# Reading expert and batch numbers one at a time in a LoRA and top-2 MoE kernel

## The chip, the cores and the metric

The kernel runs on one core of one Trainium2 chip. The metric is the device time of one execution in microseconds (us); lower is better. It is given as the median of several executions. One more execution was recorded by the hardware profiler, and all durations below come from it.

## The reference

`x` is [16 batches, 128 rows, 128 features], `cond_8` is [16, 8]. The first layer adds to x a linear layer plus a mixture of eight rank-16 adapters weighted by `cond_8`. The second is a mixture of eight gated MLPs (128 to 512 to 128), of which each batch takes the two with the largest softmax weight, plus a shared one:

```python
x = x + (x @ W_base.T + b_base + 2.0 * lora(x, As, Bs, w=cond_8))

def _gemma_mlp(x, gate_w, up_w, down_w):
    g = jnp.einsum('bsh,hi->bsi', x, gate_w)
    u = jnp.einsum('bsh,hi->bsi', x, up_w)
    return jnp.einsum('bsi,ih->bsh', jax.nn.gelu(g, approximate=True) * u, down_w)

rw = softmax(cond_8)
w, sel = top_k(rw, 2); w = w / w.sum()
dense_w = zeros((16, 8)).at[arange(16)[:, None], sel].add(w)
moe = sum(dense_w[:, e] * _gemma_mlp(x, skill_gate[e], skill_up[e], skill_down[e]) for e in range(8))
out = x + moe + _gemma_mlp(x, shared_gate, shared_up, shared_down)
```

## The kernel before

The program writes each engine's instruction stream by hand, and the engines meet only through counting semaphores. Which batch goes to which expert is known only on the chip. The kernel therefore sorts the 32 pairs (batch, expert) into a list, `idx`, in on-chip memory: entries 0 to 31 are expert numbers, entries 32 to 63 batch numbers. VectorE writes it (L758) and then raises the semaphore `lists_ready` to 2. An engine that needs such a number reads it into a register: `down_at` (L229, an expert number times a stride) and `batch_at` (L232). In the trace each such read is a TENSOR_LOAD on the engine's own instruction sequencer, followed by register operations and an assertion.

The work comes in this order.

1. Setup and the first layer.
2. The shared MLP over four groups of four batches (`shared_group(g)`, L969). Step `c` of a group makes one 128-wide piece of gate and up (`gate_up_shared`, six matmuls of 512 columns) and then the down product of two pieces earlier (`down_shared`, three matmuls). In the last group TensorE reads four expert numbers, `first`, after the last gate and up.
3. Four "singles" (pairs that found no partner): `gate_up_single(s)` is 16 matmuls, `down_single(s)` is eight and needs the expert number `first[s]`. TensorE reads four more numbers, `last`, for the four singles at the very end, two before `down_single(1)` and two before `down_single(2)`.
4. Twelve "slots", each two batches of one expert. Slots 0 to 2 are written out, 3 to 11 are a loop of three turns (L1101). A slot has two halves, n = 0 and n = 1. In each half TensorE does `gate_up_slot` (12 matmuls of 256 columns) and then `down_slot` of the same half of the slot before (six).
5. Four last singles, the merge of the sums, and the output.

Tile t is one half of a slot. ScalarE takes its gelu (L533) and later rounds the product to its high part (L542). VectorE multiplies gelu and up (`gated`, L697), and then subtracts to get the low part (`split_h_lo`, L714). In half n it does `gated(t)` first and then `split_h_lo(t - 1)`. `down_slot` of a half waits for that half's low part (`lo_done`, L1040). So in half 1 of slot p TensorE waits for the split that VectorE makes in half 0 of slot p, and in half 0 of slot p + 1 for the split made in half 1 of slot p. VectorE also reads the two batch numbers of the previous slot in half 0 (`where`, L791), after the split, and adds that slot's result in half 1 (`add_slot`, L780).

SyncE copies the gate and up weights of a slot from `wex` to `wst`, both in on-chip memory, 1024 KB at a time (L284), once the slot three before has left its buffer.

VectorE's stream around the first singles is `gated_single(1)`, `add_single(0)`, two reads, `gated_single(2)`, `add_single(1)`, two reads, `gated_single(3)`, `add_single(2)`, `add_single(3)`, two reads, and then slot 0. `down_single(s)` waits for `gated_single(s)`.

Of the kernel before, what the change touches and what calls it, by code (L numbers as in the profile page):

```python
# [17 lines left out]
def lora_then_top2_moe(nc, x, cond, W_base, b_base, As, Bs, ex_gate, ex_up, ex_down,  # L18
# [8 lines left out]

    B, S, H = x.shape
    E, _, I = ex_gate.shape
    R = As.shape[1]  # L30
    P = 128
    assert S == P and H == P and E * R == P and I == 512
    GB = I // S
    NG = B // GB
    NC = I // P
# [4 lines left out]
    NU = NG * NC  # L40
    NP = 12
    NF, NL = 4, 4
    NS = NF + NL
    PB = NU + NF
    LB = PB + 2 * NP
    LEFT = 2 * NP
    NBUF = 3
    RT_WEIGHTS = 11

    with ExitStack() as ctx:  # L50
# [3 lines left out]
        def sem(name):  # L54
            return ctx.enter_context(nc.semaphore(name))
# [127 lines left out]
        lists_ready = sem("lists_ready")  # L183
# [39 lines left out]
        def split_count(t):  # L223

            return t + (1 - NF)

        def down_at(eng, n):

            return eng.snap(eng.value_load(idx[0:1, bass.ds(n, 1)], min_val=0, max_val=E - 1) * DN)  # L229

        def batch_at(eng, n):
            return eng.value_load(idx[0:1, bass.ds(n + 32, 1)], min_val=0, max_val=B - 1)  # L232
# [373 lines left out]
        def _(dve):  # L606
# [86 lines left out]
            def gated(t, q, u):  # L693

                dve.wait_ge(up_done, t + 1)
                dve.wait_ge(gelu_done, t + 1)
                dve.tensor_tensor(up_ps[u][:, :], up_ps[u][:, :], gelu_sb[q], ALU.mult).then_inc(h_done, 1)  # L697

            def gated_single(s):
                t = SINGLES[s]  # L700
                dve.wait_ge(up_done, t + 1)
                dve.wait_ge(gelu_done, t + 1)
                if s >= 2:
                    dve.wait_ge(down_done, SINGLES[s - 2] + 1)
                dve.tensor_tensor(h_sb[t % 2], up_ps[t % 3][:, :], gelu_sb[t % 2], ALU.mult).then_inc(h_done, 1)  # L705

            def split_h_lo(t, q, u, count):

                dve.wait_ge(hi_done, count)
                if isinstance(t, int) and PB <= t < PB + 2:  # L710
                    dve.wait_ge(down_done, NU)
                elif not (isinstance(t, int) and t < 2):
                    dve.wait_ge(down_done, t - 1)
                dve.tensor_tensor(hT_lo[:, q, :], up_ps[u][:, :], f32(hT_hi[:, q, :]), ALU.subtract).then_inc(lo_done, 1)  # L714
# [56 lines left out]
            def batches_of(p):  # L771
                return [batch_at(dve, 2 * p + n) for n in range(2)]

            def add_slot(p, j, where):

                dve.wait_ge(down_done, 2 * p + (PB + 2))
                dve.wait_ge(acc_done, 2 * p + NF)
                for n in range(2):
                    of_b = total[:, bass.ds(where[n], 1), :].rearrange("p a s -> p (a s)")
                    dve.scalar_tensor_tensor(of_b, slot_ps[j][:, n * S:(n + 1) * S], wlist[:, bass.ds(2 * p + n, 1)],  # L780
                                             of_b, ALU.mult, ALU.add).then_inc(acc_done, 1)

            def slot(p, j):
                adds = not (isinstance(p, int) and p == 0)
                for n in range(2):
                    t = 2 * p + (PB + n)
                    gated(t, n, (PB + 2 * j + n) % 3)
                    if adds or n == 1:
                        split_h_lo(t - 1, 1 - n, (PB + 2 * j + n - 1) % 3, split_count(t - 1))
                    if adds and n == 0:  # L790
                        where = batches_of(p - 1)  # L791
                    if adds and n == 1:
                        add_slot(p - 1, (j + 2) % NBUF, where)

# [19 lines left out]
            gate_lo(E - 1)  # L814
            sum_group(NG - 1)
            first = [batch_at(dve, LEFT + s) for s in range(2)]
            gated_single(1)
            add_single(0, first[0])
            first += [batch_at(dve, LEFT + s) for s in range(2, NF)]
# [2 lines left out]
            last = [batch_at(dve, LEFT + s) for s in range(NF, NF + 2)]  # L822
            gated_single(3)
            add_single(2, first[2])
            add_single(3, first[3])
            last += [batch_at(dve, LEFT + s) for s in range(NF + 2, NS)]
            dve.wait_ge(sum_done, NG)
            for p in range(NBUF):
                slot(p, p)
            with dve.Fori(1, NP // NBUF) as i:  # L830
                for j in range(NBUF):
                    slot(NBUF * i + j, j)
            where = batches_of(NP - 1)
            split_h_lo(LB - 1, 1, (LB - 1) % 3, split_count(LB - 1))
            gated_single(NF)
            add_slot(NP - 1, (NP - 1) % NBUF, where)
            gated_single(NF + 1)
            for g in range(NG):
                merge(g)
# [8 lines left out]
        def _(pe):  # L848
# [101 lines left out]
            def down_shared(g, c):  # L950

                q = c % 2
                pe.wait_ge(lo_done, NC * g + (c + 1))
                if c == 0:
                    if isinstance(g, int) and g == 0:
                        pe.wait_ge(x1_ready, 2)
                        pe.wait_ge(sh_dlo, 1)
                    else:
                        pe.wait_ge(sum_done, g)
                w_hi = wshd[:, 0, c, :]  # L960
                w_lo = wshd[:, 1, c, :]
                pe.matmul(shared_ps[:, :], w_hi, hT_hi[:, q, :], start=(c == 0), stop=False)  # L962
                pe.matmul(shared_ps[:, :], w_hi, hT_lo[:, q, :], start=False, stop=False)
                pe.matmul(shared_ps[:, :], w_lo, hT_hi[:, q, :], start=False, stop=(c == NC - 1)  # L964
                          ).then_inc(down_done, 1)

            first = []

            def shared_group(g):  # L969
                for c in range(NC):  # L970
                    gate_up_shared(g, c)
                    if NC * g + c == NU - 1:
                        pe.wait_ge(lists_ready, 2)
                        first.extend(down_at(pe, LEFT + s) for s in range(NF))
                    if g == 0 and c == 2:
                        sort_starts()
                    if g == 1 and c == 2:
                        sort_singles()
                    if g == 2 and c == 3:
                        sort_lists()  # L980
                    if c >= 2:
                        down_shared(g, c - 2)
                    elif g > 0:
                        down_shared(g - 1, c + 2)

            def gate_up_single(s):

                t = SINGLES[s]
                j = s % NBUF
                pe.wait_ge(xs_ready, s + 1)  # L990
                pe.wait_ge(st_gu[j], 32 * (s // NBUF) + 32)
                pe.wait_ge(h_done, t - 1)
                if s < 3:
                    pe.wait_ge(lo_done, t - 2)
                elif NF <= s < NF + 3:
                    pe.wait_ge(lo_done, split_count(t - 3))
                for k, ps, done in ((0, gate_ps[t % 2], gate_done), (1, up_ps[t % 3], up_done)):
                    for c in range(NC):
                        mm = pe.matmul(ps[:, c * S:(c + 1) * S], sst[:, j, k * I + c * P:k * I + (c + 1) * P],  # L999
                                       xs[:, s % NBUF, :], start=True, stop=True)  # L1000
                    mm.then_inc(done, 1)

            def down_single(s, e0):

                t = SINGLES[s]
                if s in (2, 3):
                    pe.wait_ge(acc_done, s - 1)
                elif s == NF + 1:
                    pe.wait_ge(merged, 3)
                elif s == NF + 2:  # L1010
                    pe.wait_ge(res_done, 1)
                elif s == NF + 3:
                    pe.wait_ge(merged, NG)
                pe.wait_ge(h_done, t + 1)
                for c in range(NC):
                    mm = pe.matmul(single_ps[s][:, 0:H], h_sb[t % 2][:, c * S:(c + 1) * S],  # L1016
                                   wexd[:, bass.ds(e0 + c * H, H)], start=(c == 0), stop=(c == NC - 1))
                mm.then_inc(down_done, 1)
# [66 lines left out]
                shared_group(g)  # L1085
            pe.wait_ge(ld_down, 32)
            gate_up_single(0)
            down_shared(NG - 1, NC - 2)
            down_shared(NG - 1, NC - 1)
            gate_up_single(1)  # L1090
            down_single(0, first[0])
            gate_up_single(2)
            last = [down_at(pe, LEFT + s) for s in range(NF, NF + 2)]
            down_single(1, first[1])
            gate_up_single(3)
            last += [down_at(pe, LEFT + s) for s in range(NF + 2, NS)]
            down_single(2, first[2])
            down_single(3, first[3])
            for p in range(NBUF):
# [46 lines left out]
```

## Time and profile before

| | |
|---|---|
| median of 3 executions | 135.22 us (134.91 to 135.67) |
| the profiled execution | 135.5 us, span from first to last instruction 133.8 us |
| TensorE matmul busy | 127.2 us, 95% of the span, 869 matmuls |
| VectorE busy | 88.7 us, 66% |
| ScalarE busy | 70.9 us, 53% |
| GpSimd busy | 60.2 us, 45% |
| granted TensorE clock, whole span | 1.00 (2.4 GHz) |

The span leaves out 1.7 us of the execution's own 135.5 us. Matmul intervals overlap in the records: a matmul of 256 columns lasts 0.28 us, but in an undisturbed row the next one starts 0.12 us after it, one of 512 columns 0.23 us. So an idle TensorE is best seen from the distance between two starts. Register reads are not counted as busy time of any engine; they stand in the chain as DVEq (VectorE's sequencer) or, where the profile names nothing, as "issue".

### The profile page before, as it was taken

The numbers are of one execution on the slowest core, as the hardware profiler recorded it, in microseconds if no ns is written. First come the engines' busy times: TensorE is split into PE (matmuls) and PEld (weight loads), VectorE is DVE, ScalarE is ACT, GpSimd is POOL, SyncE is SP. The second block draws the span as 40 slices with busy tenths as digits, with TensorE's granted clock in tenths as the row PEclk, the third lists the DMA queues.
The fourth block names the chain that finished last, engine by engine and source line by source line (L and its number), as shares of the span: only waits on it lengthen the run. The fifth ranks groups of instructions, "written<-read, shape, count | busy, mean of one in ns | idle before, by whom it ended". The sixth has DMA issues, their size and how long they took to land.

```text
span 133.8 us, 3280 instructions
## 1 busy us (share of the span) xinstructions
PE 127.2 (95%) x869; PEld 114.2 (85%) x869; DVE 88.7 (66%) x172; ACT 70.9 (53%) x134; POOL 60.2 (45%) x110
## 2 busy tenths in 40 slices
PE   6899999999999989996999999999999999999991
PEld 6658787878878869995999999999989999989991
DVE  2668978779977888533376658656855686756732
ACT  3432867976876766120466485657554755711110
POOL 5209384497777644632064543554255504610000
DMA  3898878798000185599345686558799940013822
GB/s 51 245 335 290 287 197 300 227 308 247 12 2 0 39 266 170 157 394 409 144 174 218 238 316 240 193 201 313 260 316 322 347 167 0 0 41 121 248 85 61
DMA packets 14526, 26.56 MB, mean 199 GB/s; under 512 B 2225, under 2 KB 7601, under 8 KB 12977
## 3 DMA queue, kind: packets, MB, share of 16 engines
q1 hardware_dynamic: 14192, 26.35, 58.8%
q8 instruction: 5, 0.08, 0.2%
q10 hardware_dynamic: 320, 0.07, 0.2%
q14 instruction: 9, 0.07, 0.2%
HBM read 12.52 MB, written 1.31 MB: 103 GB/s over the span
## 4 chain that ended last, share of the span: by engine, by line
PE 78%; DVEq 6%; DVE 4%; issue 4%; DMA 3%; ACT 2%; SPq 0%; ACTq 0%
PE bank L999 8%; PE bank L1036 7%; PE bank L1035 7%; PE bank L1034 7%; PE bank L946 5%; PE bank L948 5%; PE bank L947 5%; DVEq L232 5%; PE bank L1016 5%; PE bank L1056 4%; PE bank L962 3%; PE bank L1058 3%; PE bank L1057 3%; PE bank L871 3%; PE bank L964 3%
## 5 line engine op out<-in xcount | busy, mean ns | idle before, releaser
L533 ACT ACTIVATE work<-bank 128x512 f32<-128x512 f32 x48 | 28.7, 598 | 43.0 <-PE bank L1036 18.3
L697 DVE TENSOR_TENSOR bank<-bank,work 128x512 f32<-128x512 f32 x40 | 27.9, 697 | 23.2 <-PE bank L1036 12.5
L714 DVE TENSOR_TENSOR hT_lo<-bank,hT_hi 128x512 fp32r<-128x512 f32 x40 | 27.3, 682 | 1.7 <-issue 0.8
L1034 PE MATMUL bank<-xp,wst 128*128 128x256 f32 x96 | 27.2, 284 | 0.0
L1035 PE MATMUL bank<-xp,wst 128*128 128x256 f32 x96 | 27.2, 283 | 0.0
L1036 PE MATMUL bank<-xp,wst 128*128 128x256 f32 x96 | 27.1, 283 | 0.0
L463 POOL TENSOR_TENSOR wstd<-wexd,wstd 128x512 fp32r<-128x512 f32 x12 | 15.5, 1295 | 23.8 <-ACT wstd L575 23.8
L542 ACT CAST hT_hi<-bank 128x512 fp32r<-128x512 f32 x40 | 23.3, 582 | 2.4 <-DVE bank L697 1.3
L1035 PEld LDWEIGHTS bank<-xp,wst 128*128 128x128 f32 x96 | 18.4, 192 | 0.0
L1036 PEld LDWEIGHTS bank<-xp,wst 128*128 128x128 f32 x96 | 18.4, 192 | 0.0
L1034 PEld LDWEIGHTS bank<-xp,wst 128*128 128x128 f32 x96 | 18.4, 192 | 0.0
L999 PE MATMUL bank<-xs,sst 128*128 128x128 f32 x128 | 15.6, 275 | 0.0
L999 PEld LDWEIGHTS bank<-xs,sst 128*128 128x128 f32 x128 | 15.1, 192 | 0.2
L1056 PE MATMUL bank<-hT_hi,wstd 128*128 128x256 f32 x48 | 14.4, 301 | 0.6 <-DVE hT_lo L714 0.5
L456 POOL CAST xp<-x1s 128x256 fp32r x24 | 9.6, 398 | 11.1 <-issue 10.1
L1058 PE MATMUL bank<-hT_hi,wstd 128*128 128x256 f32 x48 | 13.6, 283 | 0.0
L1057 PE MATMUL bank<-hT_lo,wstd 128*128 128x256 f32 x48 | 13.6, 282 | 0.0
L371 POOL TENSOR_TENSOR wex<-raw_ex,wex 128x512 fp32r<-128x512 f32 x8 | 10.3, 1288 | 6.3 <-DVE wex L719 6.3
L946 PE MATMUL bank<-x1s,wsh 128*128 128x512 f32 x32 | 12.6, 393 | 0.0
L948 PE MATMUL bank<-x1s,wsh 128*128 128x512 f32 x32 | 12.5, 390 | 0.0
L947 PE MATMUL bank<-x1s,wsh 128*128 128x512 f32 x32 | 12.5, 389 | 0.0
L705 DVE TENSOR_TENSOR work<-bank,work 128x512 f32<-128x512 f32 x8 | 5.5, 690 | 8.4 <-PE bank L999 5.8
(146 smaller groups left out, 212.7 us busy)
## 6 DMA issues: line engine op xcount, KB each, us to landing
wst<-wex SPq DMA_DIRECT2D x12, 1024.0 KB, 5.0
raw_ex<-n_L_cond_skill_gate_dram SPq DMA_DIRECT2D x8, 256.0 KB, 3.3
raw_ex<-in_L_cond_skill_up_dram SPq DMA_DIRECT2D x8, 256.0 KB, 4.2
sst<-n_L_cond_skill_gate_dram SPq DMA_DIRECT2D x8, 256.0 KB, 3.4
sst<-in_L_cond_skill_up_dram SPq DMA_DIRECT2D x8, 256.0 KB, 4.2
xn<-in_x_dram SPq DMA_DIRECT2D x4, 256.0 KB, 4.6
out_dram<-xT SPq DMA_DIRECT2D x4, 256.0 KB, 2.7
sst<-_L_cond_shared_gate_dram SPq DMA_DIRECT2D x1, 256.0 KB, 4.6
```

Source lines behind the costliest of these rows:

```text
L533: act.activation(gelu_sb[q], gate_ps[q][:, :], ACT.Gelu_apprx_tanh).then_inc(gelu_done, 1)
L542: act.copy(hT_hi[:, q, :], up_ps[u][:, :]).then_inc(hi_done, 1)
L697: dve.tensor_tensor(up_ps[u][:, :], up_ps[u][:, :], gelu_sb[q], ALU.mult).then_inc(h_done, 1)
L714: dve.tensor_tensor(hT_lo[:, q, :], up_ps[u][:, :], f32(hT_hi[:, q, :]), ALU.subtract).then_inc(lo_done, 1)
L946: pe.matmul(ps[:, :], w_hi, x1_hi(g), start=True, stop=False)
L947: pe.matmul(ps[:, :], w_hi, x1_lo(g), start=False, stop=False)
L948: pe.matmul(ps[:, :], w_lo, x1_hi(g), start=False, stop=True).then_inc(done, 1)
L999: mm = pe.matmul(ps[:, c * S:(c + 1) * S], sst[:, j, k * I + c * P:k * I + (c + 1) * P], xs[:, s % NBUF, :], start=True, stop=True)
L1034: pe.matmul(of_c, w_hi, x_hi, start=True, stop=False)
L1035: pe.matmul(of_c, w_hi, x_lo, start=False, stop=False)
L1036: mm = pe.matmul(of_c, w_lo, x_hi, start=False, stop=True)
L1056: pe.matmul(ps, w_hi, h_hi, start=(c == 0), stop=False)
```

## The change

The numbers read and the arithmetic are the same. Only the places of the reads in two instruction streams move.

- TensorE, last shared group: in place of four reads after the last `gate_up_shared`, one read after each of the steps c = 1, 2 and 3 (with the wait for the list in front of the first), and the fourth after `gate_up_single(0)`.
- TensorE, singles: the four reads of `last` stand one each after `gate_up_single(1)`, `down_single(0)`, `gate_up_single(2)` and `down_single(1)`.
- VectorE, slots 1 to 11: the first of the two reads of `where` moves from behind `split_h_lo` to between `gated` and `split_h_lo` of half 0. The second stays behind the split.
- VectorE, ends: the last two reads of `last` move from before slot 0 into slot 0, half 0, behind `gated`. The two reads for the last slot (`last_slot`) move from behind the loop into slot 0, half 1.

```diff
@@ VectorE, slot(p, j) @@
                     gated(t, n, (PB + 2 * j + n) % 3)
+                    if adds and n == 0:
+                        where = [batch_at(dve, 2 * p - 2)]
                     if adds or n == 1:
                         split_h_lo(t - 1, 1 - n, (PB + 2 * j + n - 1) % 3, split_count(t - 1))
                     if adds and n == 0:
-                        where = batches_of(p - 1)
+                        where.append(batch_at(dve, 2 * p - 1))
+                    elif n == 0:
+                        last.extend(batch_at(dve, LEFT + s) for s in range(NF + 2, NS))
+                    elif not adds:
+                        last_slot.extend(batches_of(NP - 1))
@@ VectorE, around the slots @@
+            last_slot = []
             gated_single(1)
...
             add_single(3, first[3])
-            last += [batch_at(dve, LEFT + s) for s in range(NF + 2, NS)]
...
-            where = batches_of(NP - 1)
             split_h_lo(LB - 1, 1, (LB - 1) % 3, split_count(LB - 1))
             gated_single(NF)
-            add_slot(NP - 1, (NP - 1) % NBUF, where)
+            add_slot(NP - 1, (NP - 1) % NBUF, last_slot)
@@ TensorE, shared_group(g) @@
                     gate_up_shared(g, c)
-                    if NC * g + c == NU - 1:
-                        pe.wait_ge(lists_ready, 2)
-                        first.extend(down_at(pe, LEFT + s) for s in range(NF))
+                    if g == NG - 1 and c >= 1:
+                        if c == 1:
+                            pe.wait_ge(lists_ready, 2)
+                        first.append(down_at(pe, LEFT + c - 1))
@@ TensorE, singles @@
             gate_up_single(0)
+            first.append(down_at(pe, LEFT + NF - 1))
             down_shared(NG - 1, NC - 2)
             down_shared(NG - 1, NC - 1)
             gate_up_single(1)
+            last = [down_at(pe, LEFT + NF)]
             down_single(0, first[0])
+            last.append(down_at(pe, LEFT + NF + 1))
             gate_up_single(2)
-            last = [down_at(pe, LEFT + s) for s in range(NF, NF + 2)]
+            last.append(down_at(pe, LEFT + NF + 2))
             down_single(1, first[1])
+            last.append(down_at(pe, LEFT + NF + 3))
             gate_up_single(3)
-            last += [down_at(pe, LEFT + s) for s in range(NF + 2, NS)]
             down_single(2, first[2])
```

## Rows read from the trace of the kernel before

**Rows 1.** The page, part 1: busy time and share of the span.

```profile
PE 127.2 (95%) x869; PEld 114.2 (85%) x869; DVE 88.7 (66%) x172; ACT 70.9 (53%) x134; POOL 60.2 (45%) x110
```

**Rows 2.** Timeline of TensorE: start, length, [idle before, releaser].

```profile
44.78 0.39 PE L962 MATMUL bank<-hT_hi,wshd 128*128 128x512 f32 x1
...
49.52 0.49 PE L962 MATMUL bank<-hT_hi,wshd 128*128 128x512 f32 x1 [0.50 <-issue]
...
61.51 1.15 PE L1016 MATMUL bank<-wexd,work 128*128 x8 [0.72 <-issue]
63.01 1.15 PE L1016 MATMUL bank<-wexd,work 128*128 x8 [0.34 <-DVE work L705]
```

**Rows 3.** Timeline of VectorE at the list's last write.

```profile
44.17 0.20 DVE L758 CAST idx<-bank 1x64 int32<-1x64 f32 x1
```

**Rows 4.** TensorE's first read, by its source line: durations in ns.

```profile
L229 PEldq TENSOR_LOAD <-idx x1: 493/493/493, 46.5 to 46.5; - x1
```

**Rows 5.** The chain that ended last, from 56 us on: start, length, what.

```profile
59.51 0.83 DVEq L232
...
60.65 1.00 DVEq L232
...
62.06 0.70 DVE work L705
...
118.38 0.70 DVE hT_lo L714
```

**Rows 6.** Stretches from slot start to slot start: slots 1, 2, 3 to 9, 10, 11.

```profile
66.87:71.45 4.58, 4.56 (x38) 4.36 (x37) 2.58 (x4) 3.31 (x7) 3.18 (x4) 1.00 0.58 224
71.45:75.85 4.40, 4.40 (x39) 4.38 (x37) 3.04 (x7) 2.66 (x5) 2.10 (x3) 1.00 0.65 244
75.85:107.32 31.47, 31.10 (x254) 30.44 (x253) 21.02 (x42) 19.18 (x35) 14.59 (x21) 1.00 0.75 269
107.32:111.95 4.63, 4.58 (x39) 4.38 (x37) 3.52 (x7) 2.67 (x5) 1.72 (x2) 1.00 0.28 108
111.95:116.27 4.32, 4.32 (x39) 4.32 (x37) 3.09 (x7) 2.75 (x5) 1.48 (x2) 1.00 0.00 0
```

**Rows 7.** Timeline of all engines in slot 3, which starts at 75.85.

```profile
77.57 0.70 DVE L697 TENSOR_TENSOR bank<-bank,work 128x512 f32<-128x512 f32 x1
...
78.18 0.68 DVE L714 TENSOR_TENSOR hT_lo<-bank,hT_hi 128x512 fp32r<-128x512 f32 x1
...
79.45 0.28 PE L1056 MATMUL bank<-hT_hi,wstd 128*128 128x256 f32 x1
```

**Rows 8.** VectorE's reads of slot 3 (first) and from 109.3 on: min/median/max ns.

```profile
L232 DVEq TENSOR_LOAD <-idx x1: 955/955/955, 78.2 to 78.2; - x1
...
L232 DVEq TENSOR_LOAD <-idx x6: 299/304/313, 109.6 to 117.7; - x6
```

**Rows 9.** ScalarE's seven reads in slots 3 to 9: min/median/max ns.

```profile
L229 ACTq TENSOR_LOAD <-idx x7: 344/674/922, 77.1 to 103.9; - x7
```

**Rows 10.** DMA busy tenths from 75 to 90 us, 0.375 us a digit.

```profile
DMA  9700009989996200299998995100099989994100
```

**Rows 11.** The chain through VectorE's reads of slot 9.

```profile
104.89 0.08 DVEq L232
105.01 0.96 DVEq L232
...
106.38 0.77 DVEq L232
...
107.62 0.07 DVE bank L697
```

**Rows 12.** Timeline of TensorE at the last down_slot.

```profile
118.65 0.28 PE L1058 MATMUL bank<-hT_hi,wstd 128*128 128x256 f32 x1
119.13 0.39 PE L1056 MATMUL bank<-hT_hi,wstd 128*128 128x256 f32 x1 [0.20 <-DVE hT_lo L714]
119.35 0.28 PE L1057 MATMUL bank<-hT_lo,wstd 128*128 128x256 f32 x1
```

## Prediction, written before the changed kernel ran

> **What bounds the kernel now.** I read the page first. TensorE's products are 95% of the span [rows 1], and the granted clock is 1.00 in every stretch of rows 6 (last three columns: clock, DMA share, GB/s). So TensorE sets the end, and a reading counts only where TensorE stands still or comes late. I then went through TensorE's timeline for starts farther apart than 0.23 us (512 columns) or 0.12 us (256), and followed each gap back along the chain.
>
> Three kinds of gap touch the reads. In the last shared group a product starts at 49.52 after 0.50 idle, released by "issue" [rows 2]: TensorE's sequencer was reading four numbers. Its first read starts at 46.5 [rows 4], so four reads took 3.0 us, and products issued before them covered 2.3 of it. At 61.51 there are 0.72 idle for the same reason, and at 63.01 0.34 more, this time released by VectorE's L705. In the chain VectorE does nothing from 59.51 to 62.06 but two reads of 0.83+ and 1.00 us [rows 5]. In the slots, a slot takes 4.32 us when nothing is late (slot 11) and 4.58, 4.40, 31.47 / 7 = 4.50 and 4.63 in slots 1, 2, 3 to 9 and 10 [rows 6]. The excess sits in half 0, where `down_slot` waits for the low part. The last is at 119.13, 0.48 after its neighbour instead of 0.12 [rows 12].
>
> A read's price: its load takes 0.30 us from 109 us on, but 0.955 in slot 3 [rows 8]. Seven first reads of slots 3 to 9 are all long, with a mean of 0.92; the last is the 0.96 of rows 11. The DMA tenths are 9 from 77.3 to 79.9, 81.4 to 84.4 and 86 to 89 us [rows 10]. These are SyncE's 1 MB copies inside on-chip memory, one a slot, and VectorE's first read falls into each. Around the load come 0.12 us before (104.89 to 105.01) and 0.47 after it until the next operation (106.38 + 0.77 = 107.15 to 107.62) in the loop [rows 11]; in written-out code it is 61.65 to 62.06 = 0.41 after it [rows 5].
>
> **TensorE's first read.** The list is ready at 44.17 + 0.20 = 44.37 [rows 3]. The new first read stands ahead of the product due at 44.78 [rows 2] and waits for the list. With TensorE's first load of 0.49 [rows 4] and about 0.41 around it, that product starts at 45.27, 0.49 late. Removed is the gap at 49.52: 0.50 idle plus the 0.16 by which a record of 0.39 outlasts the spacing of 0.23, so 0.66. Each of the two gaps also costs some 0.10 of restart (119.13 to 119.35 is 0.22, not 0.12 [rows 12]), which cancels. Gain **0.17**. Bounds: 0 if the first load takes 0.66, and 0.36 if it takes 0.30.
>
> **TensorE's other seven reads.** I cost them at nothing: each stands behind products already issued, the old run shows that 2.3 us of such cover exists, and a read at its longest is 1.0 + 0.4 = 1.4 us. Without the cover each costs 0.7 to 1.4.
>
> **The middle of the singles.** All of the 0.72 at 61.51 should turn into waiting. `down_single(3)` needs VectorE's L705, which stands behind the two reads from 59.2 to 62.06. Those start when `down_single(1)` is done, which TensorE's own later reads don't move. So the product of 63.01 comes earlier by 0.17 alone, and the 0.88 (0.72 + 0.16) freed before it is spent standing there. Gain **0**; at best about 1.2, if VectorE's two loads fell to 0.3.
>
> **Slots 0 and 1.** VectorE gets four new reads here. Two, behind `gated` in half 0, lie in the time in which ScalarE makes the next gelu: nothing. The other two begin around 67.4 (estimate: slot 1 starts at 66.70, its product ends 0.16 later, and ScalarE's rounding takes another 0.5). Two short reads of 0.30 + 0.41 end at 68.8. Then comes slot 1's own first read, which now stands before the split: 0.92 + 0.41 gives 70.1, and the low part 0.68 + 0.05 later gives 70.85. TensorE wants it at 66.70 + 3.60 + 0.3 (the old wait of half 0, which stays) = 70.6. With restart and the 0.05 that the first half slips, this is a loss of **0.38**. Bounds: 0, and 1.4 if the two reads are long too. Slot 2 (written out, so 0.06 shorter per read) has about 0.05 of lateness and 0.10 of restart where it had 0.08: loss **0.07**.
>
> **Slots 3 to 9, the step that decides.** In half 0 VectorE now does gated, read, split, read. Before, gated started at 77.57, the split at 78.18, and TensorE used that split's result at 79.45 without waiting [rows 7]. After: the load starts at 77.57 + 0.12 = 77.69, inside the copy [rows 10]; + 0.92 + 0.47 = 79.08 for the split; + 0.68 + 0.05 (118.38 + 0.70 = 119.08 to 119.13 [rows 5, 12]) = 79.81. That is 0.36 late, plus 0.10 restart, so 0.46 a slot. The split had 79.45 - 78.18 - 0.73 = 0.54 of slack, and its delay is 0.90. In return the pair of reads starts about 0.5 earlier, gated of half 1 is no later against TensorE, and the old waits of half 0 go. 7 x 0.46 = 3.22 against the old excess 31.47 - 7 x 4.32 = 1.23: loss **1.99**. The copy is issued when half 1's products are done, so TensorE's new wait brings it 0.46 earlier into the slot. The first read stays inside it, and the second may come out of it.
>
> **Slots 10, 11 and the tail.** No copy runs, loads are 0.30 [rows 8], and the split is then 0.28 late, inside the 0.54. Slot 10 loses its excess: gain 4.63 - 4.32 = **0.31**. At the end the split at 118.38 no longer stands behind two reads; 0.36 of gap and 0.10 of restart go: gain **0.46**. TensorE is busy from there to the last single, so both are kept.
>
> **Sum** against the profiled execution: -0.17 + 0.38 + 0.07 + 1.99 - 0.31 - 0.46 = +1.50, so 135.5 + 1.5 = 137.0. The median shown stands 0.28 below that execution: **136.7**, 1.1% more.
>
> **Bounds of the first read.** Nothing in the trace shows VectorE reading that early in a slot. ScalarE reads at 77.1, as the copy begins: 0.34 to 0.92, median 0.67 [rows 9]. With 0.67 a slot costs 0.11 + 0.10 = 0.21 and the sum is about -0.25. With the 1.00 of rows 5 it is about +2.2. I take 0.92, because 77.69 lies as deep in the copy as rows 10 can show.
>
> The Trainium skill (DMA: Bandwidth & Descriptors, Latency and other measured facts) gives a register load a floor of about 600 ns. The 0.30 of rows 8 lies under that floor, so the trace disagrees. By 0.6 in every slot the split would be hardly late, the estimated sum about -1, and the time 134.2.
>
> **Rivals.**
> - The stand-apart works. The early read is short (under 0.92 - 0.36 = 0.56), the split keeps its slack, and the waits of half 0 go: 0.17 + 0.46 + 0.31 + 1.23 + 0.08 = 2.25 less, 133.0. For: loads of 0.30 exist, and ScalarE's shortest is 0.34. Against: seven of seven long. The change pays from a read under about 0.71.
> - The same end by another mechanism: what follows a read need not wait for it. Against: L705 starts at 62.06, right behind a read whose number it does not use [rows 5].
>   The Trainium skill (Advanced Engine Details and Errata, Sequencer Loop) says that other engine instructions can be read and queued while the sequencer executes a control instruction, which would give that. I give it 3 in 100, within the chance of the first rival.
> - Near no change, 135.2: the early read costs like ScalarE's 0.67, or VectorE's two reads in the singles become quick once TensorE does not read beside them (both near 1.0 there), which gives 1.2 back. Against: loads are as long in the slots, with TensorE not reading.
> - Worse, 138: slots 0 and 1 see four long reads in a row (+1.0).
>
> **How the numbers follow.** Forecast (136.0 to 137.6) 0.59, worse 0.08, near no change 0.15, faster 0.18. A measurement tells some 0.5% (0.7 us) from nothing. Slower is the first two, 0.67; same 0.15; faster 0.18. The range is 134.4 to 137.9: it leaves out most of the fast rival and half of the worst one. The forecast's own range is 136.0 to 137.6.
>
> **What would show it.** In the new trace: VectorE's L714 of half 0 starting about 1.5 after L697, not 0.6; TensorE's waits at L1056 in half 1, once a slot, some 0.4, and none in half 0; slots 3 to 9 at 4.78 each; the product near 44.8 coming 0.5 late and none late at 49.5; a wait of 1.4 before `down_single(3)`; no gap at the last `down_slot`. I am wrong if the first load of a slot is short, or if L714 starts while the load still runs.

## The result and the profile after

The changed kernel takes 137.22 us (median of 4, 136.88 to 137.33) against 135.17 us before (4 executions). The ratio is 1.0143, 95% interval 1.012 to 1.0166. The change makes the kernel 1.4% slower; 136.7, 1.1% slower, was forecast. The profiled execution took 137.23 us and has a span of 135.5 us, 1.7 more than before.

The slots come first. These are the same stretches as in [rows 6], from slot start to slot start: slots 1, 2, 3 to 9, 10, 11. The columns are length, busy time of PE, PEld, DVE, ACT and POOL, granted clock, DMA share, GB/s.

```profile
66.73:71.58 4.85, 4.83 (x38) 4.43 (x37) 2.89 (x5) 3.32 (x7) 3.19 (x4) 1.00 0.56 216
71.58:76.06 4.48, 4.48 (x39) 4.38 (x38) 3.51 (x7) 2.67 (x5) 2.09 (x3) 1.00 0.62 234
76.06:109.82 33.76, 32.01 (x254) 30.59 (x253) 22.30 (x43) 18.83 (x35) 14.39 (x21) 1.00 0.73 257
109.82:114.14 4.32, 4.32 (x38) 4.32 (x37) 3.27 (x7) 2.67 (x5) 1.54 (x2) 1.00 0.16 61
114.14:118.46 4.32, 4.32 (x38) 4.32 (x37) 3.20 (x7) 2.74 (x5) 1.65 (x3) 1.00 0.00 0
```

Slots 3 to 9 grew from 31.47 to 33.76 us, and slot 10 shrank from 4.63 to 4.32. The clock is 1.00 throughout, so nothing here is a throttle.

Next, two places on the chain that ended last (start, length, what): VectorE's reads in the singles, which [rows 5] show before, and slot 3, which [rows 7] show.

```profile
59.30 0.91 DVEq L232
...
60.51 1.00 DVEq L232
...
61.93 0.70 DVE work L705
...
77.77 0.08 DVE bank L697
77.85 0.04 issue
77.89 0.98 DVEq L232
...
79.38 0.70 DVE hT_lo L714
80.08 0.04 issue
80.12 0.39 PE bank L1062
```

In slot 3 the read's load starts 0.12 after gated, lasts 0.98, and the split starts 0.51 after its end. L714 now starts 1.61 behind L697, where it was 0.61. The split's product L1062 (L1056 before) starts at 80.12.

TensorE's timeline at the same places, at those of [rows 2], and at the end as in [rows 12]:

```profile
45.23 0.49 PE L967 MATMUL bank<-hT_hi,wshd 128*128 128x512 f32 x1 [0.36 <-DVE hT_lo L714]
...
49.43 0.39 PE L967 MATMUL bank<-hT_hi,wshd 128*128 128x512 f32 x1
...
60.41 1.06 PE L1022 MATMUL bank<-wexd,work 128*128 x8
62.87 0.82 PE L1022 MATMUL bank<-wexd,work 128*128 x5 [1.40 <-DVE work L705]
...
79.53 0.28 PE L1042 MATMUL bank<-xp,wst 128*128 128x256 f32 x1
80.12 0.39 PE L1062 MATMUL bank<-hT_hi,wstd 128*128 128x256 f32 x1 [0.32 <-DVE hT_lo L714]
80.35 0.28 PE L1063 MATMUL bank<-hT_lo,wstd 128*128 128x256 f32 x1
...
120.85 0.28 PE L1064 MATMUL bank<-hT_hi,wstd 128*128 128x256 f32 x1
120.96 0.28 PE L1062 MATMUL bank<-hT_hi,wstd 128*128 128x256 f32 x1
```

- The product at 80.12 was due 0.12 after its neighbour, at 79.65. It is 0.47 late. The next one follows after 0.22 (the lines are rounded) in place of 0.12, which adds the 0.10 of restart. So slot 3 loses 0.57.
- The gap at 49.5 is gone, and one at 45.2 has come. The releaser named there, L714, is not the cause: TensorE's first load runs from 44.33 to 44.82 in the trace, in front of this product.
- The gap of 0.72 at 61.5 is gone, and the one behind it grew from 0.34 to 1.40. It ends when L705 does, behind VectorE's two reads.
- At the end the two products follow each other at 0.12; the 0.46 is won.

The seven first loads of slots 3 to 9 last 0.91 to 0.98, mean 0.94. The view of L714's source line tells who waited for it in that stretch (us, times):

```profile
  PEld bank L1062: 3.2, 7
  PE bank L1062: 1.8, 7
```

These are seven waits, one a slot. All lie in half 1: the late products start at 80.12, 84.94, 89.75, 94.57, 99.38, 104.16 and 109.00, each 0.49 to 0.59 after its neighbour instead of 0.12.

### The profile page after: what moved, and what is told of

It is laid out like the page before. It is cut to its first block, busy times and chain, and to the rows that moved or that the text cites. A ratio compares the mean times of both kernels' runs of the same rounds, so it can differ in the third digit from the quotient of the medians.

```text
span 135.5 us, 3280 instructions
## 1 busy us (share of the span) xinstructions
PE 127.4 (94%) x869; PEld 114.2 (84%) x869; DVE 91.0 (67%) x172; ACT 70.6 (52%) x134; POOL 60.1 (44%) x110
## 4 chain that ended last, share of the span: by engine, by line
PE 71%; DVEq 8%; DVE 8%; ACT 4%; issue 4%; DMA 1%; POOL 1%; ACTq 0%; POOLq 0%
PE bank L1005 9%; DVEq L232 8%; PE bank L953 5%; PE bank L951 5%; PE bank L952 5%; PE bank L1022 5%; PE bank L1062 5%; PE bank L1042 5%; PE bank L1040 5%; PE bank L1041 5%; DVE hT_lo L714 4%; PE bank L967 3%; ACT work L533 3%; PE bank L1063 3%; PE bank L1064 3%
## 5 line engine op out<-in xcount | busy, mean ns | idle before, releaser
L697 DVE TENSOR_TENSOR bank<-bank,work 128x512 f32<-128x512 f32 x40 | 28.0, 699 | 15.9 <-PE bank L1042 6.6
L714 DVE TENSOR_TENSOR hT_lo<-bank,hT_hi 128x512 fp32r<-128x512 f32 x40 | 27.4, 685 | 8.3 <-issue 7.1
L1062 PE MATMUL bank<-hT_hi,wstd 128*128 128x256 f32 x48 | 14.7, 306 | 1.8 <-DVE hT_lo L714 1.8
L1062 PEld LDWEIGHTS bank<-hT_hi,wstd 128*128 128x128 f32 x48 | 9.1, 190 | 3.7 <-DVE hT_lo L714 3.6
```

Source lines behind the costliest of these rows:

```text
L1062: pe.matmul(ps, w_hi, h_hi, start=(c == 0), stop=False)
```

## The experiments

Each is compared with the kernel before on the same chip. A ratio below 1 is faster than before. Experiments 9 and 10 ran on another chip than the rest: the kernel before took 135.42 us there, against 135.27 beside experiments 1, 2, 3 and 6 and 135.18 beside 4, 5, 7 and 8. In the quoted expectations, `one_each` is experiment 7, `one_each_singles` is 8 and `scalar_early` is 9.

**1. The change with the slots' two reads put back.**

```diff
-                    if adds and n == 0:
-                        where = [batch_at(dve, 2 * p - 2)]
                     if adds or n == 1:
                         split_h_lo(...)
                     if adds and n == 0:
-                        where.append(batch_at(dve, 2 * p - 1))
+                        where = batches_of(p - 1)
```

> The changed kernel, with both batch reads of a slot again behind the split (only the reads around the slots and TensorE's reads stay moved). Theory: the whole loss is the first read of a slot standing ahead of the split, inside SyncE's copy. Then slots 3 to 9 return to about 31.5 us (33.8 in the changed kernel), slot 10 to about 4.6, the end keeps its 0.46 and the opening its 0.14: about 134.6 us. Rival: the four reads put into slot 0 or TensorE's reads cause the loss; then the slots stay at 4.8 each and the time near 137.

Measured: 134.87 us, ratio 0.9974 (0.9957 to 0.999), against 134.6 expected. Slots 1, 2, 3 to 9 and 10 take 4.59, 4.38, 31.33 and 4.57, the lengths of [rows 6] within 0.15. So the rest of the change is a small gain (0.40 us in the medians), and the loss is the place of one read.

**2. The kernel before with that one read moved.**

```diff
+                    if adds and n == 0:
+                        where = [batch_at(dve, 2 * p - 2)]
                     if adds or n == 1:
                         split_h_lo(...)
                     if adds and n == 0:
-                        where = batches_of(p - 1)
+                        where.append(batch_at(dve, 2 * p - 1))
```

> The kernel before, with one edit: the first of a slot's two batch reads moves between gated and split in half 0. Theory: this edit alone makes slots 3 to 9 take about 33.8 us in place of 31.5, with TensorE's waits in half 1, and slot 10 0.3 shorter: about 137.2 us. Rival: the loss needs the other moves as well; then 135.2.

Measured: 137.61 us, ratio 1.0191 (1.0141 to 1.0241). Its stretches of slots 2, 3 to 9 and 10:

```profile
71.28:76.12 4.84, 4.57 (x38) 4.36 (x37) 3.15 (x7) 2.67 (x5) 2.35 (x4) 1.00 0.58 223
76.12:109.86 33.74, 32.01 (x254) 30.59 (x253) 22.30 (x43) 18.80 (x35) 14.13 (x21) 1.00 0.72 258
109.86:114.18 4.32, 4.32 (x38) 4.32 (x37) 3.30 (x7) 2.67 (x5) 1.54 (x2) 1.00 0.15 56
```

33.74 is the changed kernel's 33.76. The edit alone makes the whole loss. (One of the four executions took 139.04; the other three lie between 137.09 and 137.72.)

**3. TensorE's reads alone.** TensorE's stream is the changed one, all other engines are as before (the two TensorE hunks of the diff above).

> The kernel before, with TensorE's reads moved as in the change and VectorE as before. Theory: the gap at 49.5 us becomes one near 45 that is only 0.1 to 0.2 shorter, and the gap at 61.5 turns into waiting for VectorE: about 135.0 us. Rival: TensorE's reads were on the path, and the freed 0.66 + 0.88 comes through: about 133.6.

Measured: 135.24 us, ratio 1.0003 (0.9987 to 1.0018), 12 executions. TensorE's waits from 44 to 66 us:

```profile
PE bank L1017 <- DVE work L705: 1.4, 1, 1.4
PE bank L962 <- DVE hT_lo L714: 0.3, 1, 0.3
```

Seven of eight reads left the path and nothing came through: the time stands at `down_single` (L1017), in front of VectorE's L705. The short wait at L962 is again TensorE's first load, from 44.26 to 44.76, whatever releaser the line names.

**4. No copies beside the reads.** SyncE's copies for slots 3 to 11 are left out, so those slots compute with the weights of slots 0 to 2.

```diff
+                if p >= NBUF:
+                    return
                 w0 = sp.snap(expert_at(2 * p) * GU)
@@ TensorE @@
-                        pe.wait_ge(st_w[j], 16 * turn + 16)
+                        pe.wait_ge(st_w[j], 16)
```

> The changed kernel without SyncE's on-chip copies of gate and up weights for slots 3 to 11 (nine of twelve; those slots compute with the weights of slots 0 to 2, so part of the result is left out). Theory: the register loads are long only because these copies run. Without them each load takes 0.3 us from slot 1 on, the early read leaves the split in its 0.54 of slack, and slots 3 to 9 take 4.32 each: about 133.4 us with TensorE's waits of half 1 gone. Rival: the early read is long by its place (a neighbour's load, VectorE's busy pipeline); then loads stay near 0.9 and the time near 137.

Measured: 133.17 us, ratio 0.9857 (0.9835 to 0.988). VectorE's reads from 68 us to the end of the slots, by their source line:

```profile
L232 DVEq TENSOR_LOAD <-idx x23: 298/302/323, 67.8 to 112.7; - x23
```

No load is long any more, and slots 2 to 11 take 4.32 each, with the read still ahead of the split. The load itself is 0.30 to 0.32 in the first read of every slot from 1 to 11. SyncE's own reads for those copies are gone too, but they are no rival: in the changed kernel each took 0.26 to 0.28 and had ended 1.3 us or more before VectorE's began.

DMA traffic as such is not enough to make a load long. In the kernel before, the only transfers from 54.60 to 54.91 us are 256 KB loads from outside into on-chip memory. They keep the DMA share at 0.96 and move 370 GB/s, and a load of VectorE took 0.31 there. Beside the first copies, from 58.64 to 59.61, the share is 1.04 and the rate 405 GB/s, and a load of TensorE took 0.97. The output writes at 126 us move only 287 GB/s, and SyncE's loads beside them took 0.80 and 0.64. What the slow cases share, and the fast one lacks, is that the DMA reads on-chip memory. Which part of that path is shared was not tried.

**5. The dose: both reads ahead of the split.**

```diff
-                        where = [batch_at(dve, 2 * p - 2)]
+                        where = batches_of(p - 1)
...
-                        where.append(batch_at(dve, 2 * p - 1))
+                        pass
```

> The changed kernel with both reads of a slot between gated and split in half 0. Theory: what a read holds up beyond 0.54 us comes out one for one. The second read adds 0.7 (load 0.3) to 1.2 us to the split's delay in slots 3 to 9, and slots 10 and 11, which had slack, now wait 0.4 each too: slots 3 to 9 between 5.4 and 6.0, slots 10 and 11 near 4.8, 143 to 148 us. Rival: only the presence of a read there costs (a fixed restart); then under 139.

Measured: 144.88 us, ratio 1.0722 (1.0694 to 1.075). Slots 3 to 9 take 5.23 to 5.73 each (38.5 in all), slots 10 and 11 4.88. Two of the seven slots lie under the expected 5.4, the total time inside the expected 143 to 148. In slot 7 L714 starts 2.47 behind L697:

```profile
100.91 0.70 DVE L697 TENSOR_TENSOR bank<-bank,work 128x512 f32<-128x512 f32 x1 [0.66 <-PE bank L1042]
103.38 0.69 DVE L714 TENSOR_TENSOR hT_lo<-bank,hT_hi 128x512 fp32r<-128x512 f32 x1 [1.77 <-issue]
```

The split is 2.47 - 0.61 = 1.86 late, and less the 0.54 of slack this gives 1.32. Slot 7's product is late by 1.32 (it starts 1.44 after its neighbour, not 0.12). So the delay beyond the slack comes out one for one. Slots 10 and 11, with their short loads, bound the slack: two reads of 0.3 exceed it, one does not.

**6. Both reads in half 1.**

```diff
                     if adds and n == 1:
-                        add_slot(p - 1, (j + 2) % NBUF, where)
+                        add_slot(p - 1, (j + 2) % NBUF, batches_of(p - 1))
```

The two reads of half 0 are taken out.

> The changed kernel, with both batch reads of a slot in half 1, behind that half's split and just ahead of the two adds that use them. Theory: there no copy runs, so the loads take 0.3 us, they end before the adds could start anyway, and neither split stands behind a read: all slots near 4.32 us and about 133.0 us. Rival: the pair of reads delays the adds and, through them, gated and split of the next half 0; with loads of 0.9 the pair takes 2.6 us, the split comes 0.8 late, and the time is above 137.

Measured: 134.84 us, ratio 0.9968 (0.9948 to 0.9987): neither number. The loads did become short (median 0.30, longest 0.56), as the theory had it. The rest is mostly the rival's mechanism in two places, 0.73 in slot 6 and 0.50 at the end. TensorE's timeline:

```profile
92.60 0.38 PE L1060 MATMUL bank<-hT_hi,wstd 128*128 128x256 f32 x1 [0.47 <-DVE hT_lo L714]
...
118.12 0.39 PE L1060 MATMUL bank<-hT_hi,wstd 128*128 128x256 f32 x1 [0.24 <-DVE hT_lo L714]
```

The chain before 92.60 runs from ScalarE's read, late that turn, through VectorE's two reads, the two adds and the loop's branch to the split. Slot 6 takes 5.05 in place of 4.32. At 118.12 the same order costs the end 0.50 (0.40 late and 0.10 of restart), which takes back the 0.46 that the change had won.

**7. One read behind each split.**

```diff
                     if adds and n == 0:
-                        where.append(batch_at(dve, 2 * p - 1))
+                        where = [batch_at(dve, 2 * p - 2)]
                     if adds and n == 1:
+                        where.append(batch_at(dve, 2 * p - 1))
                         add_slot(p - 1, (j + 2) % NBUF, where)
```

The read ahead of the split is taken out.

> The changed kernel with one batch read of a slot behind the split of half 0 and the other behind the split of half 1. Theory: the first, long (1.3 us in all), ends before half 1's product is done, and the second, short, ends about when the adds can start. No split and no adds come late: slots 2 to 11 near 4.32, the end keeps its 0.46, about 133.5 us. Rival: the read in half 1 still delays adds and loop branch, as both did in the run with two reads there; then some slot shows a wait of 0.3 to 0.6 and the time is 134.5 or more.

Measured: 133.18 us, ratio 0.9857 (0.9836 to 0.9878). Stretches of slots 2, 3 to 9 and 10:

```profile
71.23:75.55 4.32, 4.32 (x38) 4.32 (x37) 3.17 (x7) 2.67 (x5) 2.10 (x3) 1.00 0.64 245
75.55:105.79 30.24, 30.24 (x254) 30.24 (x253) 22.23 (x43) 19.00 (x35) 14.58 (x21) 1.00 0.76 275
105.79:110.11 4.32, 4.32 (x38) 4.32 (x37) 3.09 (x7) 2.67 (x5) 1.55 (x2) 1.00 0.46 152
```

PE busy equals the length: no wait is left in these slots, although the reads of half 0 are as long as ever (0.87 to 0.96 in slots 1 to 9).

**8. Also VectorE's reads in the singles.**

```diff
-            last = [batch_at(dve, LEFT + s) for s in range(NF, NF + 2)]
             gated_single(3)
+            last = [batch_at(dve, LEFT + s) for s in range(NF, NF + 2)]
```

> As one_each, and VectorE's two long reads ahead of gated_single(3) moved behind it. Theory: TensorE's wait of some 1.6 us before down_single(3) is those two reads (with TensorE's own reads already out of the way); gated_single(3) can start at its gelu, about 1.4 earlier: 132.1 us. Rival: another wait takes its place (the adds of singles 2 and 3, or slot 0's product that needs them), and less than 0.5 comes through.

Measured: 132.18 us, ratio 0.978 (0.976 to 0.9801). Slot 0 starts at 62.55 in place of 63.69, but slot 1 takes 5.05 in place of 4.59, so 0.46 of it is given back. The gain in the trace is thus 1.14 - 0.46 = 0.68, while the medians show 1.00. That the median meets the expected 132.1 is partly luck. The theory took 1.4 from the 133.5 expected of experiment 7, which itself came out at 133.18, and it had no loss in slot 1. The profiled execution was the slowest of five (132.51). ScalarE's read for slot 0 now falls into the last of the first copies:

```profile
L229 ACTq TENSOR_LOAD <-idx x1: 946/946/946, 63.7 to 63.7; - x1
```

**9. Also ScalarE's first read ahead of the slots.**

```diff
             act.wait_ge(lists_ready, 2)
+            e0_first = down_at(act, 0)
             for p in range(NBUF):
```

> As one_each_singles, and ScalarE's read for slot 0 (now 0.95 us long, between two gelus of slot 0) moved ahead of the slots, where ScalarE has some 3 us of idle time. Theory: the wait of 0.76 that appeared in slot 1's half 0 is that read; slot 1 returns to 4.6 or less, 131.7 us. Rival: VectorE's four reads in slots 0 and 1 cause it; then 132.2.

Measured: 131.92 us, ratio 0.9746 (0.9718 to 0.9773). Slot 1 is back at 4.60. The read was the cause of most of that wait; the wait of some 0.3 that slot 1 had before is still there.

**10. Also TensorE's first two reads behind step c = 2.**

```diff
-                    if g == NG - 1 and c >= 1:
-                        if c == 1:
+                    if g == NG - 1 and c >= 2:
+                        if c == 2:
                             pe.wait_ge(lists_ready, 2)
+                            first.append(down_at(pe, LEFT))
                         first.append(down_at(pe, LEFT + c - 1))
```

> As scalar_early, and TensorE's first two reads both behind step c = 2 of the last shared group, none behind c = 1. Theory: at c = 1 the list is not written when the sequencer arrives, and so the read has no cover; behind c = 2 nine products stand issued ahead of it, and the gap of 0.66 near 45 us goes: 0.7 less than scalar_early, 131.0 us. Rival: the sum that the next down product waits for (sum_done) or the loads of the first single take the gap's place, and less than 0.3 comes through.

Measured: 131.7 us, ratio 0.9717 (0.969 to 0.9744). In the trace the gap is gone. It was 0.49 there (45.10 in experiment 9, due at 44.61), plus 0.10 of restart, and not 0.66. From the list's product (L911) to slot 0 it is 40.10 to 62.07 = 21.97, against 39.78 to 62.39 = 22.61, so 0.64 less. In the medians only 0.22 shows, within their spread. By time that is the rival's number (less than 0.3), by the trace the theory's; that this version beats number 9 is not shown by time.

## Why the prediction was right, point by point

Span against span, the terms measured as follows.

| term | forecast | measured |
|---|---|---|
| opening, to slot 0 | -0.17 | -0.13 (63.91 to 63.78) |
| slots 0 and 1 | +0.38 | +0.26 |
| slot 2 | +0.07 | +0.08 |
| slots 3 to 9 | +1.99 | +2.29 |
| slot 10 | -0.31 | -0.31 |
| the end | -0.46 | -0.46 |
| sum | +1.50 | +1.73 |

The change is slower for the forecast reason, and each term has the forecast sign and nearly its size. Only a small part of the agreement is luck: in the sum, 0.12 too much for slots 0 and 1 stands against 0.30 too little for slots 3 to 9.

- **Slots 3 to 9.** The deciding step held: the read stands ahead of the split, inside the copy, and each slot waits once in half 1. The forecast had 0.46 a slot, measured are 33.76 / 7 - 4.32 = 0.50. The load was 0.94 instead of 0.92, and the split started 0.50 to 0.51 after it and not 0.47. This is the largest error of the sum, 0.30. Experiments 1 and 2 fix the cause from both sides, and 4 and 5 fix load and slack. The prediction read the DMA tenths of [rows 10] a little too wide (the nines end at 79.5, not 79.9), which no term uses.
- **TensorE's first read.** Right in kind: it has no cover because the list is not written yet. The new gap is 0.52 (0.49 forecast) in place of the old 0.66, a difference of 0.14 (0.17 forecast); experiment 10 takes it away.
- **The middle.** Right: 0.72 idle became waiting for VectorE (0.34 to 1.40). Experiment 3 shows no gain from TensorE's reads, and experiment 8 shows that VectorE's two reads held the place.
- **Slots 0 and 1.** 0.12 less than forecast. (The forecast's own parts, 0.25 late, 0.10 of restart and 0.05 of slip, add to 0.40, where it has 0.38.) The split's product waited from 70.60, when it was due, to 70.76, since the load was 0.87. The two reads in front of it took 0.30 each, so the rival of four long reads in a row did not occur.
- **The median.** 136.7 had 0.28 taken off because the old profiled execution lay above its median. The new one (137.23) lies on its own. With the 0.23 of the sum that is the 0.5 between forecast and result.
- **The rivals.** The short early read did not occur beside a copy, and experiment 4 shows that it occurs without one: 133.2, where that rival had 133.0. "What follows a read need not wait" is refuted by the chain of slot 3, where L714 needs nothing from the read and stands behind it. ScalarE's rounding, which it does need, had ended at 78.14, 1.24 before L714 started. The Trainium skill's sentence (Advanced Engine Details and Errata, Sequencer Loop) that other instructions can be queued while a control instruction executes does not help here: whether or not L714 was queued, it did not start before the load was over, in seven slots of seven. (The page does not say whether a register load counts as a control instruction.) The rival "near no change" had two ways. The early load was 0.94 and not ScalarE's 0.67, and VectorE's two loads in the singles took 1.23 and 1.00 after the change (1.16 and 1.00 before), with no read of TensorE beside them (its last ended at 57.86).
- **The floor.** The Trainium skill's floor of about 600 ns for a register load (DMA: Bandwidth & Descriptors, Latency and other measured facts) did not hold: 23 loads of experiment 4 took 0.298 to 0.323.

## What to carry to other kernels

A register read stops its engine's stream until the number is there, also for operations that do not use it; only what was issued ahead of it goes on. Place it behind the operation with the least slack, ahead of one that is going to wait anyway, and count its time at the worst neighbour (here 1.3 to 1.6 us beside an on-chip copy, 0.7 without). Two reads in one gap and two reads one on each side of the tight operation are both worse than one read in each of two gaps: 134.9, 137.2 and 133.2 us here (experiment 1, the change, experiment 7). When a reading is taken off the busiest engine, first look which other engine's reads stand behind the same gap.

## What the runs showed of the hardware that was not expected

- A load of one number from on-chip memory takes 0.26 to 0.32 us, and some 0.8 to 1.24 when a DMA copy reads on-chip memory all the while. Loads near a copy's start or end lie between (ScalarE's 0.34 to 0.67 before the change). All five engines show it: in the changed kernel up to 1.23 on VectorE, 1.19 on GpSimd, 1.06 on SyncE and 0.92 on TensorE, and 1.18 on ScalarE in experiment 9.
- An engine's first such load is longer than its next without any copy: 0.49 on TensorE, 0.56 on VectorE, 0.48 on ScalarE, and before the change 0.50 on GpSimd and 0.47 on SyncE at 44.4 us, when the DMA engines were nearly idle (share 0.03). Later ones took 0.26 to 0.31. Why is not shown.
